# Value products that stream their columns four times, and 18 products into a free bank ahead of the attention, in a gated block on one core

## What is computed

```
x = x + tanh(g_xattn) * attention(layernorm(x), ctx, ctx)
x = x + tanh(g_ffn) * (moe(layernorm(x)) + shared(layernorm(x)))

# attention, per head:
log_D = cumsum(log_f)[s] - cumsum(log_f)[t] + ig[t]   (t <= s, else -inf)
D_mat = exp(log_D - rowmax);  C = (q @ k.T / sqrt(32)) * D_mat
h = (C / max(|sum C|, exp(-rowmax))) @ v
```

## Time and profile before

| | us |
|---|---|
| runs, median of 3 | 307.25 (306.86 to 309.63) |
| profiled execution, its own time | 307.44 |
| its span | 305.4 |
| TensorE busy in the span | 225.1 (74%) |
| VectorE busy | 195.0 (64%) |
| ScalarE busy | 142.2 (47%) |
| GpSimd busy | 141.3 (46%) |

### The profile page before, as it was taken

The page is one execution under the profiler, slowest core; times in us unless marked ns, Lnnn a source line. Parts: engine busy times, 40 slices in busy tenths (PEclk is TensorE's granted clock), DMA queues, the critical chain, the costliest instruction groups (busy, mean ns, idle before and its releaser), DMA issues.

```text
span 305.4 us, 5288 instructions
## 1 busy us (share of the span) xinstructions
PE 225.1 (74%) x1660; PEld 182.4 (60%) x1660; DVE 195.0 (64%) x454; ACT 142.2 (47%) x264; POOL 141.3 (46%) x183
## 2 busy tenths in 40 slices
PE   0378029998989979999983908958899997987200
PEld 0234018987878869888882507535688886865100
DVE  7893882466856754984409886794578733947442
ACT  2665434456454475325511386524367745754100
POOL 4896143544169509530670737572000034664772
PEclk9989755999775587555575885788999999999955
DMA  7999981355723212400150216493989998999863
GB/s 171 372 168 154 345 328 36 90 159 169 212 83 120 66 41 68 106 0 0 38 155 17 87 52 156 105 374 87 144 116 231 209 208 207 187 194 348 260 182 103
DMA packets 74395, 46.94 MB, mean 154 GB/s; under 512 B 52737, under 2 KB 68481, under 8 KB 74241
## 3 DMA queue, kind: packets, MB, share of 16 engines
q1 hardware_dynamic: 64896, 30.09, 42.4%
q0 software_dynamic: 3216, 10.49, 11.0%
q10 hardware_dynamic: 6256, 6.03, 7.7%
HBM read 20.12 MB, written 17.83 MB: 124 GB/s over the span
## 4 chain that ended last, share of the span: by engine, by line
PE 56%; DVE 12%; DMA 11%; issue 6%; POOL 4%; SPq 4%; ACT 3%; another core or an unknown queue 2%; POOLq 1%; DVEq 0%; ACTq 0%
PE bank L700 10%; PE bank L853 8%; PE bank L866 7%; DMA qT<-xs 5%; PE bank L719 3%; PE bank L675 3%; PE bank L673 3%; PE bank L671 3%; DMA x_all<-x 3%; PE bank L739 2%; PE bank L746 2%; POOL kT L614 2%; PE bank L685 2%; PE bank L637 2%
## 5 line engine op out<-in xcount | busy, mean ns | idle before, releaser
L614 POOL DMA_INDIRECT kT<-ys,slot_y x32 | 33.2, 1039 | 58.2 <-DMA ys<-heads 44.6
L700 PE MATMUL bank<-vaug,heads 128*128 128x33 f32 x256 | 43.6, 324 | 3.5 <-DVE h_sum L1296 3.5
L700 PEld LDWEIGHTS bank<-vaug,heads 128*128 128x128 f32 x256 | 42.6, 251 | 4.1 <-DVE heads L1260 4.0
L1260 DVE SCALAR_TENSOR_TENSOR heads<-bank,heads 128x512 f32<-128x512 f32 x32 | 22.0, 688 | 32.2 <-ACT heads L980 24.8
L980 ACT ACTIVATE heads<-bank 128x512 f32<-128x512 f32 x32 | 19.1, 596 | 34.3 <-PE bank L675 34.0
L853 PE MATMUL bank<-qT,w_hi 128*128 128x256 bf16 x184 | 31.5, 273 | 4.3 <-DMA qT<-xs 3.5
L525 POOL TENSOR_TENSOR w_lo<-w_stage,w_hi 128x1024 bf16<-128x1024 f32 x9 | 19.4, 2151 | 16.9 <-ACT w_hi L985 16.9
L866 PE MATMUL bank<-w_hi,h_n 128*128 x92 | 25.1, 273 | 2.2 <-issue 2.2
L1543 DVE TENSOR_TENSOR vaug<-vaug 128x512 f32<-128x512 f32 x23 | 15.9, 691 | 15.4 <-ACT vaug L1128 11.6
L866 PE MATMUL bank<-w_lo,h_n 128*128 x92 | 25.1, 272 | 0.5 <-issue 0.5
L853 PE MATMUL bank<-qT,w_lo 128*128 128x256 bf16 x92 | 25.1, 273 | 0.1
(11 more groups left out here) (248 smaller groups left out, 578.4 us busy)
## 6 DMA issues: line engine op xcount, KB each, us to landing
ys<-heads ACTq DMA_DIRECT2D x23, 256.0 KB
w_stage<-experts SPq DMA_DIRECT2D x9, 512.0 KB, 5.0
q_pad<-parts SPq DMA_DIRECT2D x36, 128.0 KB, 2.6
x_all<-x SPq DMA_DIRECT2D x4, 512.0 KB, 7.1
w_hi<-ctxT SPq DMA_DIRECT2D x4, 512.0 KB, 7.7
vaug<-ctx SPq DMA_DIRECT2D x16, 128.0 KB, 3.9
out<-x_all SPq DMA_DIRECT2D x16, 128.0 KB
parts<-kT SPq DMA_DIRECT2D x3, 512.0 KB, 5.4
```

What stands on the lines that cost most here:

```text
L614: g.indirect_dma_start(out=y_tok[:, t % GB, k, :], out_offset=None, in_=ys[0:DONE[t] * UNIT], in_offset=bass.IndirectOffsetOnAxis(ap=slot_ ...
L700: last = mm(bank[4 + c // 2][:, at:at + DV], p_sb[:, j % PS, c * P:(c + 1) * P], vaug[:, b, c, j, :], start=True, stop=True)
L1260: v.scalar_tensor_tensor(p_sb[:, j % PS, :], bank[2 + j % 2][:], SCALE, d_sb[:, j % 2, :], ALU.mult, ALU.mult).then_inc(p_ok, 1)
```

## The change

`head_values` gives the moving operand a repeat of 4 with step 0, so that each product streams 132 columns and writes the same 33 results four times side by side. The copies fall into columns that later heads of the group overwrite, or behind the group's 132; so that they stay inside the chunk's half of the bank, the two chunks of a bank now lie UNIT = 256 columns apart and not 132. `group_add` reads them from there; what it reads has the same size.

`keep_busy` sends products of the mask (512 columns, bf16, the operands of L675) into bank 1, which nothing reads: 10 after `a_ok`, 8 behind the four transposes.

```diff
+            def keep_busy(to, n):
+                for _ in range(n):
+                    mm(to[:], ident_b[:], mask[:].rearrange("p c s -> p (c s)"), start=True, stop=True)
+
...
                 for c in range(C):
-                    at = (c % 2) * GV + (j % 4) * DV
-                    last = mm(bank[4 + c // 2][:, at:at + DV], p_sb[:, j % PS, c * P:(c + 1) * P],
-                              vaug[:, b, c, j, :], start=True, stop=True)
+                    at = (c % 2) * UNIT + (j % 4) * DV
+                    last = mm(bank[4 + c // 2][:, at:at + 4 * DV].rearrange("p (r d) -> p r d", r=4), p_sb[:, j % PS, c * P:(c + 1) * P],
+                              vaug[:, b, c, j:j + 1, :].to_broadcast([P, 4, DV]), start=True, stop=True)
                 last.then_inc(pv_ok, 1)
...
+            pe.wait_ge(const_ok, 3)
+            pe.wait_ge(a_ok, 1)
+            keep_busy(bank[1], 10)
             pe.wait_ge(rows_ok, 1)
             pe.wait_ge(state_row_ok, 1)
...
             last.then_inc(rows_psum, 1)
+            keep_busy(bank[1], 8)
...
-                v.tensor_tensor(h4[:, 0:2], bank[4][:, 0:2 * GV].rearrange("p (c g) -> p c g", c=2), carried[:, 0:2], ALU.add)
-                v.tensor_tensor(h4[:, 2:4], bank[5][:, 0:2 * GV].rearrange("p (c g) -> p c g", c=2),
+                v.tensor_tensor(h4[:, 0:2], bank[4][:].rearrange("p (c g) -> p c g", c=2)[:, :, 0:GV], carried[:, 0:2], ALU.add)
+                v.tensor_tensor(h4[:, 2:4], bank[5][:].rearrange("p (c g) -> p c g", c=2)[:, :, 0:GV],
```

## The result

The changed kernel takes 293.26 us (median of 4 runs, 292.91 to 294.13) against 307.06 us for the kernel before (4 runs, 306.09 to 309.63): a ratio of 0.9543, 95% interval 0.9481 to 0.9604. The prediction was 295.5 us with a range of 287 to 303. The profiled execution took 293.27 us (span 291.5 us); the one of before 307.44 us (305.4 us). Executions of one kernel on one chip lie up to 4.5% apart in what follows, and each trace is of one of them, in experiments 2, 8 and 10 of one over 1.5% above the fastest.

What follows compares the result with a forecast made beforehand. TensorE at half clock was taken to set the pace in the attention's second half. Terms -3.4 - 1.4 - 3.9 - 5.5 = -14.2 us, +2.6 for clock falls, took 307.44 to 295.8, or 295.5 us at the median; range 287 to 303.

Steps and rivals of the forecast that it cites:

- What bounds the kernel: In the attention's second half, TensorE at 1.2 GHz sets the pace; streamed columns raise its clock, busy time does not.
- The price of a wide pass: Value products, priced by L719: 0.122 us at full clock, 0.247 at half; 0.11 or 0.30 us more a head.
- Batch 0: Attention's start: enters at full clock, saving 4.3 us, less 0.9 for eight heads' extra columns: -3.4 us.
- Batch 1: Mean of A 1.35 us earlier, then TensorE waits about 2 us for `k_wt` behind GpSimd's chain: -1.4 us.
- Batch 2: Attention at full clock: -2.6 us to product 4, then 1.3 from there to the next batch's first product: -3.9 us.
- Batch 3: Attention's end at full clock: -2.5 us to product 4, -3.0 from there to product 7: -5.5 us.
- Two falls: Allowance for the clock falling while TensorE waits for VectorE, mostly in the attention's later half: +2.6 us.
- The wait behind the attention: VectorE's 6.63 us wait after its last product, for something on no engine of this core, stays as long.
- the third rival: Wait after the last product ends with TensorE's last inter-chunk product, no clock falls: -16 to -20 us, 288 us; 20%.
- Behind it: Rest of the kernel after the attention: untouched, only moves along, no change in its length.
- The first rival: Attention's clock stays as it is, so only the wider passes' price is left: +7 us, 314 us; chance 5%.
- the second: Only the attention's start gains; later waits let the clock fall as before: 306 to 309 us, no difference; 8%.

Runs made afterwards that it cites:

- experiment 2: Changed kernel with value products back at 33 columns, the 18 mask products kept: 294.46 us, beside 297.32 for the kernel before.
- experiment 8: The changed kernel again, unedited, on another chip: 294.50 us, beside 303.61 for the kernel before.
- experiment 10: The kernel before, unedited, run again with a trace of its own: 309.74 us (two runs).
- experiment 1: Changed kernel without the 18 mask products, 132-column value products kept: 285.66 us, beside 297.32 for the kernel before.
- experiment 3: Changed kernel with two copies (66 columns) instead of four in the value products: 292.33 us, beside 297.32 for the kernel before.
- Experiment 4: 33-column value products, 18 mask products kept, plus one unused 512-column mask product ahead of each head's scores: 292.42 us, beside 297.32 for the kernel before.
- experiment 6: Changed kernel with GpSimd making the next batch's keys and the residual before the third low part: 292.66 us, ratio 0.9671 to the kernel before.
- Experiment 5: Changed kernel with 16 instead of eight mask products behind the transposes: 292.32 us, beside 303.61 for the kernel before.
- experiment 7: Changed kernel with 16 mask products behind the transposes and GpSimd's keys and residual moved earlier: 293.73 us, ratio 0.9694 to the kernel before.

## Why the prediction was right, and where its terms were off

- **What bounds the kernel** was read rightly: TensorE at half clock, because of what it streams and not of how long it is busy. Experiments 1, 2 and 3 show it: with 132-column passes batch 1 is at 1.00, with 33 at 0.67 to 0.92, and 66 stand between over the span in three of four executions (0.843 to 0.847, against 0.788 to 0.830 and 0.859 to 0.892). Experiment 4 adds columns in another place and raises the clock in all its executions.
- **The price of a wide pass.** L719's rows gave 0.122 us at full and 0.247 at half clock. Measured: (63.15 - 62.19) / 8 = 0.120 us at full clock, and in experiment 6 (93.91 - 92.02) / 8 = 0.236 at half. With 0.108 us for 33 columns that is 0.012 us more a pass, close to the lower bound of 0 and far from the upper one of 0.085; the nearest row of the same kind was the right one.
- **The 18 products**: no delay of the transposes (40.93 against 40.94), none of the decay product. Right.
- **Batch 0, -3.4 us expected, -0.45 measured.** This is the step that failed, as the prediction put it: "so I expect the attention to start at 1.00", and that it then stays. It did start so, and fell after 1.7 us, at 46.8 us. I had taken the eight products to reach 45.2 us, which holds only at half clock; at full clock (the working had that number too, 43.6 us) they end at 43.2 and leave 1.90 us idle. The clock that the first ten products had won made the next eight too short to cover the gap. Experiment 5 supports the size of the term: with the gap filled batch 0 is 19.63 us. The fall itself is no certainty with eight (experiments 6 and 8), so that the gap alone decides it is not shown.
- **Batch 1, -1.4 expected, -1.5 measured**: the group product starts at 90.27 us against 92.20, 1.93 earlier, of which 0.45 came from batch 0. TensorE waits 1.55 us there for `k_wt`, as expected (about 2), behind the GpSimd chain of the earlier trace rows.
- **Batch 2, -3.9 expected, -4.1 measured** (first product of batch 3 is 6.0 us earlier, of which 1.93 from before). To product 4 it was -1.9 instead of -2.6, from there on -2.2 instead of -1.3: the halves were mis-sized, the sum was not.
- **Batch 3, -5.5 expected, -5.9 measured** by the last product (11.9 us earlier, where 6.0 were brought along); -2.2 of it to product 4 (expected -2.5).
- **Two falls, +2.6**: the trace shows such falls, at waits of 2.77 and 1.99 us, but the batches came out as worked out without them. That falls cost nothing there is not shown: batch 2 to product 4, which holds one, gained 0.7 us less than expected, and in experiment 8, where the same program is at 0.50 from 94.9 to 101.5 us, batch 2 lasts 2.0 us longer.
- **The wait behind the attention** was to stay at 6.63 us. It is 2.95 us for TensorE's inter-chunk product, so 3.7 us more were gained than the sum has. Here the third rival's mechanism was right (it puts the end of the wait at the last inter-chunk product), and experiment 10 shows that this wait can be near 3 us in the kernel before as well (it is 1.4 to 3.9 us in all traces but the first of before). The first trace of before overstates that stage, and with it the gain of this one trace pair; the medians of four runs each still lie 13.8 us apart.
- **Behind it** 1.9 us were given back up to the first unit product (from the scaling 54.8 us before, 56.7 after), with 0.3 us regained at the end. The prediction had 0 there. The same stretch takes 53.0 to 61.7 us in the thirteen traces, and 55.1 to 58.6 us in the four of experiments 5 to 8, so 1.9 us need no cause in the change.

Together: -0.45 - 1.5 - 4.1 - 5.9 - 3.7 + 1.9 - 0.3 = -14.0, against -13.9 for the spans. The forecast was -14.2 + 2.6 = -11.6: it was 2.95 us too good in batch 0 and 1.9 behind the attention, and too careful by 3.7 at the wait and by the allowance of 2.6. The errors cancelled in part, so that the total came out nearer than its parts is luck; the mechanism and the terms of batches 1 to 3 are not. The first rival (clock stays, 314 us) and the second (the start alone pays) are out: experiment 1 has nearly the whole gain of batches 1 to 3 without the start. Why batches 2 and 3 differ by up to 3 us between traces of one program stays open; the clock alone does not say it, since batch 2 of the kernel before is longer at 0.73 (34.64 us) than at 0.65 (31.81 us). What lengthened the stage behind the attention is open as well.

## What to carry to other kernels

Where TensorE is fully busy and its clock reads 0.5, look at how many columns each weight load is followed by. If float32 weights are reloaded for few columns, streaming the same operand several times into free columns of the bank costs almost nothing (0.012 us a pass here) and can hold the clock; try one copy fewer too, since more columns than needed bring nothing (three copies did here what four do). When idle time is filled to hold the clock, size the filling by its duration at the *full* clock, and expect the gain to end at the next engine's chain: batch 0 got 3.5 us shorter with it here, and no total shows it.

## What I had not expected of the hardware

- The same program can hold or lose the clock: the changed kernel's batch 0 took 23.14 us in one trace and 21.28 in another, and 19.63 in experiment 6, whose stream on TensorE up to there is the same.
- A VectorE operation of 32 columns took 2.15 us instead of 0.21 beside a GpSimd operation of 128x1024 (experiments 6 and 7); the cost is VectorE's and shows in no wait. The kernel before has this too: L1271 and L1274 last 1.11 and 1.30 us at 94.98 and 96.12 us, beside GpSimd's L514 and L517, and 0.36 us as a rule.
- Three copies did as much as four, and two did as much in batches 0 and 1 (19.35 and 19.17 us) of the one trace there is, where TensorE hardly waits.
